# One core, transformer block: order of the first pair's keys, queries and LayerNorm rows, engine of the first low parts, filler transposes

## The reference, cut to what matters

```python
x = x + jnp.tanh(g_xattn[0]) * _L0_xattn_ref(_layernorm(x, axis=-1), ctx_4096, Wq, Wk, Wv, Wo, q_norm_w, k_norm_w)

kv = jnp.concatenate([context, latents], axis=1)          # 128 context rows, 128 latent rows per batch
q = (latents @ Wq)   # 32 heads of 128
k = (kv @ Wk)        # 8 key heads of 128
v = (kv @ Wv)
q = rms_norm(q, q_norm_w)
k = rms_norm(k, k_norm_w)
scores = jnp.einsum('bhgqd,bhkd->bhgqk', qg, k) * scale   # 4 query heads share a key head
probs = jax.nn.softmax(scores, axis=-1)
out = jnp.einsum('bhgqk,bhkd->bhgqd', probs, v)
return out @ Wo
```

## Time and profile before

| | us |
|---|---|
| median of 3 runs | 1215.84 |
| lowest, highest | 1215.38, 1218.82 |
| the profiled execution, own time | 1218.76 |
| its span, first to last instruction | 1217.0 |
| its mean granted TensorE clock | 0.989 |

### The profile page before, as it was taken

One profiled execution on the slowest core, in us unless ns is written; L12 is line 12 of the kernel. 1 busy time (PEld: TensorE's weight loads), 2 busy tenths in 40 slices (PEclk: granted clock), 3 DMA queues, 4 the chain that ended last, 5 costly groups with the idle time before them and its releaser, 6 DMA issues.

```text
span 1217.0 us, 20678 instructions
## 1 busy us (share of the span) xinstructions
PE 1172.9 (96%) x6912; PEld 1003.2 (82%) x6912; DVE 821.9 (68%) x2379; ACT 580.1 (48%) x1351; POOL 327.6 (27%) x287
## 2 busy tenths in 40 slices
PE   7999999999999999999999999999999999899994
PEld 6888888888889888888888888887787777577782
DVE  7767677666666766676676776678788878673333
ACT  5645455444545545455454555445443455433431
POOL 5403022120312312132030221203333403234531
PEclk8999999999999999999999999999999999999997
DMA  7001000000101101010110000002122213852316
GB/s 277 1 36 52 2 36 19 35 34 0 52 0 34 39 13 34 0 52 0 34 52 0 34 0 1 1 1 54 57 78 78 57 63 95 318 196 79 91 44 239
DMA packets 36266, 69.65 MB, mean 57 GB/s; under 512 B 5858, under 2 KB 22242, under 8 KB 34166
## 3 DMA queue, kind: packets, MB, share of 16 engines
q1 hardware_dynamic: 31014, 57.96, 14.0%
q0 software_dynamic: 3760, 8.40, 2.2%
q10 hardware_dynamic: 1440, 2.62, 0.6%
HBM read 60.57 MB, written 12.32 MB: 60 GB/s over the span
## 4 chain that ended last, share of the span: by engine, by line
PE 59%; DVE 20%; issue 9%; ACT 5%; DMA 3%; POOL 3%; SPq 1%; DVEq 0%; ACTq 0%; POOLq 0%
PE bank L374 14%; PE bank L376 14%; PE bank L375 14%; PE bank L2043 5%; PE bank L1904 3%; ACT probs L822 3%; DVE probs L1196 3%; PE bank L1747 2%; PE bank L2055 2%; DVE iq L1361 2%; DVE k_junk L1151 2%; DVE row_max L1169 2%; DVE pt_lo L1183 2%; POOL k_rstd L613 1%; PE bank L1689 1%
## 5 line engine op out<-in xcount | busy, mean ns | idle before, releaser
L822 ACT ACTIVATE probs<-bank,exp_bias,q_rstd 128x256 f32<-128x256 f32 x256 | 141.0, 561 | 136.4 <-DVE exp_bias L1177 136.4
L1188 DVE TENSOR_TENSOR o_lo<-bank,o_hi 128x512 fp32r<-128x512 f32 x64 | 44.3, 692 | 180.0 <-ACT o_hi L815 180.0
L374 PE MATMUL bank<-wkv_hi,kv_src_lo 128*128 128x256 f32 x512 | 146.2, 286 | 1.6 <-DVE kv_src_lo L1221 1.6
L376 PE MATMUL bank<-wkv_hi,kv_src_hi 128*128 128x256 f32 x512 | 146.0, 285 | 0.0
L375 PE MATMUL bank<-wkv_lo,kv_src_hi 128*128 128x256 f32 x512 | 145.8, 285 | 0.0
L617 POOL TENSOR_TENSOR q_rstd<-q_var,minus_half 128x8 f32<-128x8 f32 x32 | 52.4, 1637 | 301.9 <-DVE q_var L1156 301.9
L811 ACT ACTIVATE pt_hi<-bank 128x512 fp32r<-128x512 f32 x128 | 69.6, 596 | 116.4 <-PE bank L1747 116.4
L374 PE MATMUL bank<-wo_hi,o_lo 128*128 128x512 f32 x256 | 105.0, 410 | 1.6 <-DVE o_lo L1188 1.2
L374 PE MATMUL bank<-wq_hi,kv_src_lo 128*128 128x512 f32 x256 | 102.9, 402 | 1.3 <-issue 1.3
L376 PE MATMUL bank<-wo_hi,o_hi 128*128 128x512 f32 x256 | 102.1, 399 | 0.0
L375 PE MATMUL bank<-wo_lo,o_hi 128*128 128x512 f32 x256 | 101.5, 396 | 0.0
(11 more groups left out here) (272 smaller groups left out, 3043.4 us busy)
## 6 DMA issues: line engine op xcount, KB each, us to landing
weights<-r_w SPq DMA_DIRECT2D x16, 768.0 KB, 9.3
wq_raw<-wq SPq DMA_DIRECT2D x8, 1024.0 KB, 4.8
wo_raw<-wo SPq DMA_DIRECT2D x8, 1024.0 KB, 4.8
wkv_raw<-wkv SPq DMA_DIRECT2D x8, 512.0 KB, 3.3
y_back<-y_dram SPq DMA_DIRECT2D x8, 512.0 KB, 6.5
gu_raw<-w_gate SPq DMA_DIRECT2D x10, 256.0 KB, 3.4
gu_raw<-w_up SPq DMA_DIRECT2D x10, 256.0 KB, 3.9
wd_raw<-w_down SPq DMA_DIRECT2D x10, 256.0 KB, 4.2
```

The source lines that it names most:

```text
L374: eng.matmul(out_ap, a_lo, b_hi, start=start, stop=False)
L376: return eng.matmul(out_ap, a_hi, b_hi, start=False, stop=stop)
L822: act.activation(probs[:, h, :], scores_ps[h // 2][:, (h % 2) * 256:(h % 2) * 256 + 256], ACT.Exp, bias=exp_bias[:, h:h + 1], scale=q_rstd ...
L1188: dve.tensor_tensor(o_lo[:, par, :], o_ps[:, :], o_hi[:, par, :].bitcast(F32), ALU.subtract)\
```

## The change

- GpSimd no longer makes the first keys' weights' low parts (two instructions) and one of the four of the queries' weights; VectorE does (`first_wkv_low`, `first_wq_low(R - 1)`).
- TensorE: 5 more filler transposes between rows 0 and 1 and 14 behind row 1 (`keep_clock`). Both key halves of the first pair come ahead of rows 2 and 3. Rows 4 and 5 come behind the turned keys and first half of the queries. Rows 6 and 7 leave the start and come behind the scores of batch 1 in the loop; batch 1 now waits for low parts 4 and 5 only, and for 6 and 7 ahead of batch 0's value products.
- VectorE: the key sums come ahead of value and row low parts of the second batches, with statistics of x tiles 4 and 5 apart from each other; statistics, rows and low parts of the last pairs move into the loop (low parts of 4 and 5, statistics and rows of 6 and 7 behind the bias of batch 0, low parts of 6 and 7 behind the bias of batch 1).
- ScalarE: the first key half's copy ahead of the second context copy, context copies 2 and 3 later, high parts of rows 6 and 7 in batch 1 of the loop, ahead of its exponentials.
- GpSimd: the key root one place earlier, a new wait for row 5 (the sixth) ahead of the context low part of pair 1, and the roots of rows 6 and 7 behind the last context low part.

The diff, whole but for unchanged context:

```diff
--- before.py
+++ after.py
@@ -595,8 +595,8 @@
                     pool.tensor_tensor(wkv_lo[:, rows, :], wkv_raw[:, rows, :], wkv_hi[:, rows, :].bitcast(F32),
                                        ALU.subtract).then_inc(wkv_lo_ready, 1)
 
-            def wq_low(g):
-                for h in range(R):
+            def wq_low(g, heads=range(R)):
+                for h in heads:
                     cols = slice(h * HD, h * HD + HD)
                     pool.wait_ge(wq_hi_ready, g * R + h + 1)
                     pool.tensor_tensor(wq_lo[:, :, cols], wq_raw[:, :, cols], wq_hi[:, :, cols].bitcast(F32),
@@ -625,19 +625,20 @@
 
             ln_root(0)
             ln_root(1)
-            wkv_low(0)
+            wq_low(0, range(0, 2))
             ln_root(2)
             ln_root(3)
-            wq_low(0)
+            wq_low(0, range(2, 3))
             ln_root(4)
+            k_root(0)
             ln_root(5)
-            k_root(0)
+            pool.wait_ge(ln_row_ready[0], 6)
             ctx_low(1)
-            ln_root(6)
-            ln_root(7)
             q_root(0, 0)
             ctx_low(2)
             ctx_low(3)
+            ln_root(6)
+            ln_root(7)
 
             def one_group(g):
                 for b in range(0, NB, 2):
@@ -837,14 +838,13 @@
             key_source_high(0)
             key_source_high(1)
             wq_high(0)
+            kv_high(0, 0, 0)
             ctx_high(1)
-            kv_high(0, 0, 0)
+            kv_high(0, 1, 0)
             key_source_high(2)
             key_source_high(3)
-            kv_high(0, 1, 0)
             act.wait_ge(small_loaded, 64)
             act.activation(gate_rows[:, :], gate_rows[:, :], ACT.Tanh).then_inc(gates_ready, 1)
-            ctx_high(2)
             q_copy(0, range(0, 1), first_q)
             act.wait_ge(k_rstd_ready, 1)
             for i in range(4):
@@ -852,12 +852,10 @@
             q_copy(0, range(1, 2), first_q)
             act.wait_ge(head_w_ready, 1)
             k_high(0, 0)
-            q_high(0, 0, range(0, 1))
+            q_high(0, 0)
             key_source_high(4)
             key_source_high(5)
-            q_high(0, 0, range(1, 2))
-            key_source_high(6)
-            key_source_high(7)
+            ctx_high(2)
             ctx_high(3)
 
             def xt_high(t):
@@ -880,6 +878,9 @@
                         wq_high(g + 1)
                     if b % 2 == 1 and before_end(g, b, 1):
                         k_high(next_pair, par)
+                    if isinstance(g, int) and g == 0 and b == 1:
+                        key_source_high(6)
+                        key_source_high(7)
                     exps(n, b)
                     if prev:
                         o_high(n - 1, (b - 1) % 2)
@@ -1215,30 +1216,43 @@
                     tok = slice(t * P, (t + 1) * P)
                     ln_low(t, kv_src_hi[:, 1, :, tok], kv_src_lo[:, 1, :, tok])
 
+            def first_wkv_low():
+                dve.wait_ge(wkv_hi_ready, 1)
+                for rows in (slice(0, 2), slice(2, KC)):
+                    dve.tensor_tensor(wkv_lo[:, rows, :], wkv_raw[:, rows, :], wkv_hi[:, rows, :].bitcast(F32),
+                                      ALU.subtract).then_inc(wkv_lo_ready, 1)
+
+            def first_wq_low(h):
+                dve.wait_ge(wq_hi_ready, h + 1)
+                cols = slice(h * HD, h * HD + HD)
+                dve.tensor_tensor(wq_lo[:, :, cols], wq_raw[:, :, cols], wq_hi[:, :, cols].bitcast(F32),
+                                  ALU.subtract).then_inc(wq_lo_ready, 1)
+
             stats_pair(0)
             rows_pair(0)
+            first_wkv_low()
             dve.wait_ge(ctx_hi_ready, 1)
             dve.tensor_tensor(kv_src_lo[:, 0, :, 0:256], ctx_raw[:, :, 0:256], kv_src_hi[:, 0, :, 0:256].bitcast(F32),
                               ALU.subtract).then_inc(ctx_first_lo_ready, 1)
             low_pair(0)
             stats_pair(1)
+            first_wq_low(R - 1)
+            v_low(0, 0, 0)
             rows_pair(1)
-            stats_pair(2)
-            v_low(0, 0, 0)
+            dve.wait_ge(x_loaded[2], 16)
+            ln_stats_of(4, 4)
+            k_norm(0)
+            v_low(0, 1, 0)
             low_pair(1)
-            v_low(0, 1, 0)
-            k_norm(0)
-            rows_pair(2)
             dve.wait_ge(small_loaded, 64)
             dve.tensor_tensor(head_w[:, 2:3], head_w[:, 0:1], head_w[:, 1:2], ALU.mult).then_inc(head_w_ready, 1)
-            stats_pair(3)
             q_norm(0, range(0, 1))
-            rows_pair(3)
+            ln_stats_of(5, 5)
+            rows_pair(2)
             k_low(0, 0)
             q_low(0, 0, 0)
+            q_low(0, 1, 0)
             q_norm(0, range(1, 2))
-            q_low(0, 1, 0)
-            low_pair(2)
             dve.wait_ge(gates_ready, 1)
 
             def xt_low(t):
@@ -1261,6 +1275,10 @@
                         dve.wait_ge(q_rstd_ready, g * PAIRS + (b // 2 + 1))
                     bias_of(n, b)
                     if isinstance(g, int) and g == 0 and b == 0:
+                        low_pair(2)
+                        stats_pair(3)
+                        rows_pair(3)
+                    if isinstance(g, int) and g == 0 and b == 1:
                         low_pair(3)
                     if after_start(g, b, 1):
                         o_low(n - 1, (b - 1) % 2)
@@ -1781,20 +1799,25 @@
                     turn_rows(t)
 
 
-            for _ in range(20):
-                pe.transpose(y_ps[:, 0:P], ident[:, :], ident[:, :])
-            turn_pair(0)
+            def keep_clock(times):
+                for _ in range(times):
+                    pe.transpose(y_ps[:, 0:P], ident[:, :], ident[:, :])
+
+            keep_clock(20)
+            turn_rows(0)
+            keep_clock(5)
+            turn_rows(1)
+            keep_clock(14)
             kv_half(0, 0, 0)
+            kv_half(0, 0, 1)
             turn_pair(1)
-            kv_half(0, 0, 1)
             q_half(0, 0, 0)
             q_tile(0, 1, first_q)
-            turn_pair(2)
             turn_k(0)
             turn_q(0, range(0, 1))
+            turn_pair(2)
             pe.wait_ge(k_lo_ready, 1)
             turn_q(0, range(1, 2))
-            turn_pair(3)
             pe.wait_ge(ln_lo_ready[0], 4)
 
             def turn_x(t):
@@ -1811,11 +1834,13 @@
 
                     ng, np_ = (g, b // 2 + 1) if b < NB - 2 else (g + 1, 0)
                     if isinstance(g, int) and g == 0 and b == 1:
-                        pe.wait_ge(ln_lo_ready[0], NB)
+                        pe.wait_ge(ln_lo_ready[0], 6)
                     if after_start(g, b, 1):
                         turn_probs(n - 1)
                     scores(g, b, 0)
                     scores(g, b, 1)
+                    if isinstance(g, int) and g == 0 and b == 1:
+                        turn_pair(3)
                     if b == NB - 2 and last_group(g):
                         break
                     ahead = before_end(g, b - b % 2, 2)
@@ -1825,6 +1850,8 @@
                         if isinstance(g, int) and g == 0 and b < NB - 2:
                             pe.wait_ge(ctx_lo_ready, np_)
                         (kv_half, q_half)[b % 2](ng, np_, 0)
+                    if isinstance(g, int) and g == 0 and b == 1:
+                        pe.wait_ge(ln_lo_ready[0], NB)
                     if after_start(g, b, 1):
                         weigh_values(g, b - 1)
                     if ahead:
```

## The result

| | before | after |
|---|---|---|
| median, 20 runs each | 1217.51 us | 1219.31 us |
| lowest, highest | 1214.80, 1220.29 | 1216.76, 1224.83 |
| profiled execution: time, span, mean clock | 1218.76, 1217.0, 0.989 | 1218.82, 1217.1, 0.990 |

The ratio is 1.0017, 95% interval 1.0009 to 1.0025: the change costs 1.1 to 3.0 us, 1.8 between the medians. That is no difference by the bound of the prediction (3.65 us), and it has the sign and the size that were forecast (+2.0). The forecast time of 1217.8 stood on the median of three runs, 1215.84; that of twenty is 1.7 higher.

The account below looks back on a forecast made before the run. TensorE, busy 96%, bounds the kernel, but its start hangs on a chain of waits from the third x transfer. Late scores +1.15 and clock +0.85 give +2.0 us: 1217.8 against the 1215.84 median, range 1213.6 to 1220.4.

Parts of the forecast that it names:

- S: Start of batch 2's scores, 54.20 us in before; forecast 55.35, ahead of the price of the clock.
- Ahead of 19 us: Start of the kernel: moved low parts and fillers finish the query tiles at 23.1 us against 27.1, hidden by waiting.
- none of these four microseconds reaches the end: Start of the kernel: time saved on the query tiles is hidden, since VectorE cannot pass 19.02 us before x lands.
- the cover: VectorE's wait for the third x transfer until 19.02 us, hiding the start's savings; without it up to 4 us would count.
- R: End of GpSimd's first query root, 33.66 us in before; forecast 31.8, 1.85 us earlier.
- N: End of batch 0's division, 39.76 us in before; forecast 40.2, behind rows 6 and 7: gain gone and 0.45 more.
- Rival A: At batch 0's division: late rows hide under the exponentials, the 1.9 us gain arrives, 1213.9 us; chance 0.18.
- S without the clock: Batch 0's value products wait for low parts 6 and 7, starting batch 2's scores 1.15 us late.
- The clock: TensorE idles 4.6 us ahead of batch 0's transposes; likely half clock for 3 to 5 us of work costs 0.85 us.
- Rival C: Behind TensorE's gap: half clock lasts seven to nine microseconds, +4 to +5 us in all, 1220.3 us; chance 0.13.
- Rival D: Behind TensorE's gap: the clock holds, the rest as forecast, 1217.0 us; chance 0.13.
- Rival B: First query root gains more than counted and the clock holds: within 0.5 us of 1215.84; chance 0.08.

Follow-up runs that it names:

- 5: Four kernels: the 19 fillers put into before (ratio 0.9999) or taken out of after (1.0022); third x transfer asked for earlier in before (0.9992) and in after (0.9993).
- Experiment 2, division_first: After with the division of batch 0 ahead of rows 6 and 7 and of the statistics of tile 7; 1217.29 us, ratio to before 1.0000.
- gap_fillers: After with 36 filler transposes in TensorE's gap ahead of the transposes of batch 0; 1217.42 us, ratio to before 1.0003.
- after_no_fillers: After without its 19 filler transposes; 1220.16 us, ratio to before 1.0022.
- x_earlier: After with the third x transfer asked for ahead of four small transfers; 1217.76 us, ratio to before 0.9993.
- bias_first: After with GpSimd's context low part of pair 2 waiting for batch 0's bias; 1217.21 us, ratio to before 0.9999.
- division_bias_first: After with the edits of both division_first and bias_first; 1217.74 us, ratio to before 0.9997.
- port_free: division_bias_first with GpSimd's third context low part also held until batch 0's exponentials are divided; 1216.64 us, ratio to before 0.9985.
- port_free_x: port_free with the third x transfer asked for earlier, as in x_earlier; 1214.22 us, ratio to before 0.9969.

## Why the prediction was right

**The bound and the place to look** held. All that the change does is at S, and from there the 1.9 us travel through the rest unchanged.

**Ahead of 19 us.** VectorE waited for x until 18.81, the query tiles were done at 22.8 (forecast 23.1). The sentence "none of these four microseconds reaches the end" is right for the fillers in before (5); in the new order 1.14 us of what they save does. "With the cover gone up to 4 would" is wrong: the earlier transfer gave both kernels 0.9 us at the division, and what after gained beyond that at S is the clock's (5). Behind the transfer stood the queries' copy (0.58 us of waiting), and in before the values of the second key half (1.25). I had treated the cover as one wall, when it was a row of waits with little between them. And I left the fillers uncosted as part of what was covered, when in the new order they are 1.14 us at the root.

**R.** Forecast 1.85 earlier, measured 2.08 against X and 2.29 by the clock of the two executions. The 0.4 added for meetings with the roots was not needed.

**N.** This was the step on which the sign hung, and it held part by part: the bias done 2.4 us behind R (31.41 and 2.35), row 7 at R + 7.0, the division done at R + 8.3 (forecast 8.4). N moved by +0.13 against X, forecast +0.45; 0.23 of the difference is R's. Experiment 2 shows it: with rows 6 and 7 behind the division, N follows R. Rival A had to have row 7 done by R + 4.8.

**S without the clock.** Forecast +1.15, measured 0.99 (gap_fillers against before). The cause given, value products waiting for low parts 6 and 7, is the 0.89 us of waiting there. Two terms were off and cancel in part: the value products came 1.20 later than in before, not 1.55 (0.3 of it N's), and of this the waiting ahead of S took up 0.2, not 0.4.

**The clock.** Gap 4.6 forecast, 4.45 measured; a fall expected with four in five; its price 0.85 (0.5 to 1.3), measured 1.15 here and 0.7 and 1.4 in two other executions of the same instructions (5), so that the agreement to 0.3 us is in part luck. The half clock lasted about 5 us of work, the upper end of the 3 to 5, where I had leaned to the lower rows. Rival C needed six; after_no_fillers came to 5.8, at a price of 1.4. Rival D (no fall) is what gap_fillers makes of the kernel, S-X 0.99 over before: its size was right and its condition did not come.

The sum was +2.0, and came to +2.14 against X, +1.93 by the clock, +1.8 in the medians. Two errors with opposite signs, 0.16 and 0.3, lie in that. Rival B (up to +0.5) and rival A (-1.9) lie below the interval of +1.1 to +3.0, rival C (+4 to +5) above it. Rival D (+1.15) lies at its lower end: the run times do not rule it out, the granted clock of 0.50 in the trace does for the profiled execution.

**The block and the clock beside the pages.** The Trainium skill (SBUF — State Buffer, section "Who interferes with whom") was drawn on only for the query weights' part, behind the cover. Its place was 15 us later. By that section of the Trainium skill a GpSimd instruction that reads SBUF contends with a VectorE instruction that has two inputs in SBUF, and `tensor_scalar` is among the operations that can take the shared pair of ports too. The trace agrees: held were the bias, with two inputs in SBUF (0.16 against 2.35 us), and the division, a `tensor_scalar` (1.14 against 3.18). I had used only the first half of it. The Trainium skill (TensorE: Matmul & The Clock Gate, section "HAM oscillation — how this bites in real kernels") would have had the fall certain, and after 4.45 us it came. The 2.72 us on which I kept one in five for no fall were a shorter stretch, and said little about one of 4.6.

**Open.** What decides about the fall of the clock, and for how long. It fell in all four kernels with an idle stretch of 4.12 to 4.47 us (after, x_earlier, after_no_fillers, bias_first), behind 2.09 us (division_bias_first) and 2.24 (division_first), and in port_free behind 1.36 and 0.68. It did not fall in before behind 0.61 and 1.16 or at 1055.78 behind 2.72, nor in port_free_x behind the 1.36 and 0.68. Length alone does not order the short ones. No experiment separated the rest, and since each kernel has one profiled execution, the same kernel may do either.

## What to carry to other kernels

When a root or a reduction is made earlier, follow the gain through each list that it has to pass: here 2.1 us of it arrived at the division only after two rows had been put behind it, and a first 1.1 us at the next stage only after two subtractions of GpSimd had been moved off the bias and the division, by when the division was 4.3 us earlier. Work pushed out of a crowded start needs a place behind the consumer that is late, and "between the exponentials and their division" looks free only on the engine that waits. Compare marks relative to the last common event: the run times, with 5 us and more between lowest and highest, could not have told most of these kernels apart. And take more than one execution's word for what a fall of the clock costs.

## What the runs showed of the hardware

- A GpSimd subtraction of 128x1024 (2.37 to 2.41 us) that has begun holds some VectorE instructions up until it ends, however small they are: the 128x4 bias took 2.35 us beside it and 0.16 without (bias_first), the four divisions 3.18 and 1.14, a 128x128 key sum 1.03 and 0.28 (port_free). It did not hold up statistics of 128x512 (0.68 beside it and elsewhere), nor row low parts with one input in PSUM (1.28 for two). The subtraction took the same 2.4 us in all these cases.
- TensorE's clock fell to 0.50 behind idle stretches of 2.09 and 2.24 us in the middle of otherwise dense work, and stayed there for some 3 us of work. Behind 4.45 us (twice) and 4.47, in three kernels with the same instructions from there on, it stayed there for 4.3, 5.3 and 5.8 us of work.
- The landing of one and the same transfer, with the same code ahead of it, moved by 1.3 us between executions (X 18.17 to 19.47), and with it the whole start: two thirds of the effect under study.
